# Second attention of a four-stage block: row sums of the softmax on TensorE, division of the heads at the end

## The chip, the cores and the metric

The kernel runs on one core of a Trainium2 chip. The metric is the device time of one execution in microseconds (us). Before the change the median of 3 runs is 1199.65 us (1196.87 to 1201.66).

## The reference

Sixteen batches of 256 rows of width 256 pass through four stages, each added to x: an attention over 77 context rows, a feed-forward layer, a second attention, and a soft mixture of experts. Only the second attention is touched. Cut to it:

```python
q = layernorm(x) @ w_q            # 16 heads of 16 columns
k, v = split(ctx @ w_kv)          # 77 context rows
logits = q k^T * SCALE + (i - j) * w_rel[head]
attn = softmax(logits, axis=-1)   # exp(l - max) / sum
x = x + concat_heads(attn @ v) @ w_proj
```

## The kernel before

The second attention is `attention1`. It is written out without a loop: stage `f` runs from -2 to 17, and within a stage a step `t` runs from 0 to 7. One pair of heads `t` of batch `f` is handled per step; the later parts of batch `f-1` and `f-2` and the preparation of batch `f+1` and `f+2` are laid between the steps. Each engine executes its own list strictly in the order written, and semaphores tie the lists together. So the order of the work is that of the five loops at the end of each engine's block.

What happens to a batch, by function and line of the profile:

- DVE computes the layer norm (`ln.statistics`, L331; `ln.normalise`, L351, which writes `xn`), PE transposes it (`transpose_x`, L942), ACT rounds it (`transposed_x`, L1041, `xT_hi`) and DVE takes the rest (L1115, `xT_lo`). PE makes the queries from both (`queries`, L952). They go over DRAM into another layout (SP's queue, `q_dram`, `att_qs`).
- Step by step: `scores` (PE, L967, two matmuls of 154 columns into `s_bank`), `find_maxima` (DVE, L1127), `exponentials` (ACT, L1059, four activations of 77 columns into `ex`). The row sums are taken in two ways: for even steps DVE adds them up (`add_up`, L1133), for odd steps ACT's accumulator does. `invert` (DVE, L1142) takes the reciprocals of 4 sums a partition, and `weigh` (POOL, L1203 and L1204) multiplies exponentials by them into `prob` (64 of the 77 keys) and `tails` (13).
- Five units a batch (steps 0, 1, 3, 4, 6 of the next stage) move the probabilities to the other side: `transpose_p` (PE, L983, L979), `round_probs` (ACT, L1068, `pT_hi`), `split_probs` (DVE, L1148, `pT_lo`), `weigh_values` (PE, L1004). The last one makes for each of a unit's two chunks three matmuls of 256 columns: values hi with probabilities hi and lo, values lo with hi (PASSES), accumulated in the left half of one of two banks `o_bank`.
- `round_heads` (ACT, L1073) and `split_heads` (DVE, L1153) take the finished heads out of `o_bank`, `project` (PE, L1016) multiplies by `w_proj`, and `add_residual` (DVE, L1159) adds to x.

DVE's loop for a stage, cut:

```python
for t in range(HP):
    find_maxima(f, t)
    if n % 2 == 0: add_up(...)
    if t == 1: split_heads(f - 2, 1)
    if t == 2: split_queries(f + 1)
    invert(...)
    if t in UNIT_AT: split_probs(f - 1, UNIT_AT[t])
    if t == 0: transposed_x(f + 1)
    if t == 7: split_heads(f - 1, 0)
    if t == 5: add_residual(f - 2); ln.statistics(dve, f + 2)
    if t == 7: ln.normalise(dve, f + 2, xt_psum, 1)
```

Of the kernel before, what the change touches and what calls it, by code (L numbers as in the profile page):

```python
# [19 lines left out]
ALU = mybir.AluOpType  # L20
# [769 lines left out]
def attention1(nc, d, st):  # L790
# [7 lines left out]
    with ExitStack() as stack:  # L798
# [18 lines left out]
        rsum = [m.sb(f"rsum{i}", [P, 2 * NC]) for i in range(RING)]  # L817
        rinv = [m.sb(f"rinv{i}", [P, 2 * NC]) for i in range(RING)]
# [17 lines left out]
        vmain_zero = m.sem("vmain_zero")  # L836
# [7 lines left out]
        sum_ready, inv_ready, p_ready = m.sem("sum_ready"), m.sem("inv_ready"), m.sem("p_ready")  # L844
# [22 lines left out]

        def sums_added(n):
            return n // 2 + 1
# [66 lines left out]
        def _(pe):  # L936
# [50 lines left out]
            def weigh_values(g, u):  # L987
                n = UNITS * g + u
                pe.wait_ge(pt_lo, n + 1)
                if u == 0:  # L990
                    pe.wait_ge(vals_ready, VALS * (g + 1))
                    at_least(pe, ot_lo, DC * (g - 1) + 1)
                if u == 2:
                    at_least(pe, ot_lo, DC * g)
                for j in range(2):
                    o = j if u == TAIL_UNIT else CHUNKS[u][j] // 4
                    for k, (a, b) in enumerate(PASSES):
# [6 lines left out]
                        last = nc.tensor.matmul(o_bank[o][:, 0:N], values, pT[n % 2][b][0:rows, j * N:(j + 1) * N],  # L1004
                                                start=u in (0, 2) and j == 0 and k == 0,
                                                stop=k == 2 and ((u == TAIL_UNIT and j == 0) or (u == 4 and j == 1)))
# [31 lines left out]
        def _(act):  # L1038
# [12 lines left out]
            def exponentials(f, t):  # L1051
# [3 lines left out]
                if t % 2 == 0:  # L1055
                    at_least(act, sum_ready, sums_added(n - RING))
                for r in range(2 * NC):
                    total = {} if t % 2 == 0 else dict(accum_out=rsum[t % RING][:, r:r + 1])
                    last = nc.scalar.activation(ex[t % RING][:, r, :], s_bank[t % 2][:, r * SK:(r + 1) * SK], ACT.Exp,  # L1059
                                                bias=mx[t % 2][:, r:r + 1], **total)  # L1060
# [18 lines left out]
            for f in STAGES:  # L1079
                for t in range(HP):  # L1080
# [5 lines left out]
                    if t == 0 and here(f - 2):  # L1086
                        round_heads(f - 2, 1)
# [6 lines left out]
                    if t == 6 and here(f - 1):  # L1094
                        round_heads(f - 1, 0)

        @block.vector
        def _(dve):
# [31 lines left out]
            def add_up(f, t):  # L1130
                n = HP * f + t
                dve.wait_ge(ex_ready, n + 1)
                nc.vector.tensor_reduce(rsum[t % RING][:, :], ex[t % RING][:, :, :], AX, ALU.add).then_inc(sum_ready, 1)  # L1133

            def invert(f, t):
                n = HP * f + t
                if t % 2 == 0:
                    dve.wait_ge(sum_ready, sums_added(n))
                else:
                    dve.wait_ge(ex_ready, n + 1)  # L1140
                at_least(dve, p_ready, 2 * (n - RING + 1))
                nc.vector.reciprocal(rinv[t % RING][:, :], rsum[t % RING][:, :]).then_inc(inv_ready, 1)  # L1142

# [7 lines left out]
            def split_heads(g, j):  # L1151
                dve.wait_ge(ot_hi, DC * g + j + 1)
                nc.vector.tensor_tensor(oT[1][:, j, :], o_bank[j][:, 0:N], fp32_of(oT[0][:, j, :]),  # L1153
                                        ALU.subtract).then_inc(ot_lo, 1)
# [980 lines left out]
```

## Time and profile before

| | |
|---|---|
| median of 3 runs | 1199.65 us |
| the profiled execution | 1201.5 us, of which the span of its one core 1199.7 us |
| busy over the span | PE 1020.2 us (85%), DVE 883.1 (74%), ACT 751.3 (63%), POOL 470.3 (39%) |
| second attention, first to last work | about 702 to 956 us of the span |
| granted clock of TensorE, mean | 0.944 |

The table is read as follows. The share of busy time is a mean over stages with different limits; the change touches one stage, so that the stage's own rows count. Durations in the rows are those of single instructions and overlap a little with their neighbours: on DVE the next instruction starts some 0.08 us before the one ahead of it has ended in the record. So what an instruction costs its engine is the distance from its start to the next one's start. In the steady part of the stage one batch follows the other at a fixed distance, here called the turn: the distance between two batches' `split_queries`, at 766.31, 780.20 and 794.08 us of the span, is 13.88 us.

### The profile page before, as it was taken

The page shows a single profiled execution, that of the slowest core. Times are in us where ns is not written, and L with a number is a line of the kernel's source. Part 1 is how long each engine was busy: PE and PEld are TensorE (multiplying, and loading weights), DVE is VectorE, ACT ScalarE, POOL GpSimd, SP SyncE. Part 2 cuts the span into 40 slices and gives each one's busy share as a digit, 9 for nine tenths or more (in the row PEclk, how much of TensorE's full clock was granted, in tenths as well). Part 3 has the DMA queues.
Part 4 walks back from the last instruction along what each step waited for, and adds up shares of the span by engine and source line. Part 5 has one row for each costly group of instructions (what it writes and reads, how often), then busy time and mean ns, then how long its engine had stood idle before and what let it go on. Part 6 is the DMA issues. An engine that isn't in the chain of part 4 may idle for free. (4 is left out here: it accounts for less than half of the span.)

```text
span 1199.7 us, 27786 instructions
## 1 busy us (share of the span) xinstructions
PE 1020.2 (85%) x8021; PEld 977.4 (81%) x8021; DVE 883.1 (74%) x2261; ACT 751.3 (63%) x2515; POOL 470.3 (39%) x801
## 2 busy tenths in 40 slices
PE   6779999999999999799999947888888637777578
PEld 6679999999999998699999946787887627677567
DVE  3567767777776676677777747999998668986776
ACT  3467666666666666433333338999898527777774
POOL 0132232322323222112121126667676467663655
PEclk9889999999999999899999966999999959999789
DMA  7678970000000000100000035555556050000003
GB/s 216 152 134 218 145 122 0 0 0 0 0 0 0 0 0 1 32 1 0 0 0 0 0 109 150 154 157 164 154 152 171 13 110 2 1 2 1 1 18 122
DMA packets 72190, 75.04 MB, mean 63 GB/s; under 512 B 22608, under 2 KB 64436, under 8 KB 71988
## 3 DMA queue, kind: packets, MB, share of 16 engines
q1 hardware_dynamic: 71300, 73.52, 24.8%
q10 hardware_dynamic: 816, 0.66, 0.2%
q8 instruction: 32, 0.52, 0.2%
q14 instruction: 42, 0.34, 0.1%
HBM read 42.58 MB, written 31.54 MB: 62 GB/s over the span
## 5 line engine op out<-in xcount | busy, mean ns | idle before, releaser
L776 POOL TENSOR_TENSOR att_prob<-att_ex,att_rinv 128x308 f32<-128x308 f32 x128 | 89.9, 702 | 215.8 <-DVE att_rinv L679 202.4
L1059 ACT ACTIVATE att_ex<-att_s_bank,att_mx 128x77 f32<-128x77 f32 x512 | 143.1, 340 | 13.7 <-DVE att_mx L1127 12.2
L1346 ACT ACTIVATE ffn_hid<-ffn_h_bank,ffn_b 128x256 f32<-128x256 f32 x128 | 60.6, 474 | 125.3 <-DVE ffn_hT_lo L1377 65.3
L638 ACT ACTIVATE att_ex<-att_s_bank,att_mx 128x77 f32<-128x77 f32 x512 | 124.7, 332 | 11.5 <-DVE att_mx L669 11.4
L646 ACT ACTIVATE att_qT<-att_q_bank 128x256 f32<-128x256 f32 x128 | 49.1, 384 | 101.2 <-PE att_q_bank L496 100.2
L702 DVE TENSOR_TENSOR att_pT_lo<-att_t_bank,att_pT_hi 128x512 fp32r<-128x512 f32 x128 | 88.3, 690 | 32.2 <-ACT att_pT_hi L616 31.8
L1203 POOL TENSOR_TENSOR att_prob<-att_ex,att_rinv 128x256 f32<-128x256 f32 x128 | 79.8, 623 | 77.2 <-DVE att_rinv L1142 77.1
L516 PE MATMUL att_s_bank<-att_keys,att_qT 128*128 128x154 f32 x512 | 94.9, 308 | 0.0
L616 ACT CAST att_pT_hi<-att_t_bank 128x512 fp32r<-128x512 f32 x128 | 74.9, 586 | 24.4 <-PE att_t_bank L526 19.3
L540 PE MATMUL att_o_bank<-att_pT_hi,att_vals_hi 128*128 128x256 f32 x256 | 83.0, 324 | 3.0 <-DVE att_oT_lo L683 2.0
L967 PE MATMUL att_s_bank<-att_ks,att_qs 100*128 100x154 f32 x256 | 53.2, 292 | 34.3 <-ACT att_ex L1059 17.4
L1317 PE MATMUL ffn_o_bank<-ffn_w_hi,ffn_hT_hi 128*128 128x256 f32 x256 | 74.3, 290 | 7.8 <-DVE ffn_hT_lo L1377 7.8
L683 DVE TENSOR_TENSOR att_oT_lo<-att_o_bank,att_oT_hi 128x256 fp32r<-128x256 f32 x128 | 54.3, 424 | 33.1 <-ACT att_oT_hi L651 29.6
L496 PE MATMUL att_q_bank<-att_xT_hi,att_wq_hi 128*128 128x256 f32 x256 | 75.6, 295 | 2.9 <-DVE att_xT_lo L662 2.9
L526 PE MATMUL att_t_bank<-all_ident,att_prob 128*128 128x128 f32 x512 | 76.5, 272 | 0.0
L1304 PE MATMUL ffn_h_bank<-ffn_xT_hi,ffn_w_hi 128*128 128x256 f32 x256 | 72.6, 283 | 3.5 <-DVE ffn_xT_lo L1364 3.5
L967 PEld LDWEIGHTS att_s_bank<-att_ks,att_qs 100*128 100x128 f32 x256 | 42.1, 205 | 40.4 <-DMA att_qs<-q_dram 31.2
L1127 DVE TENSOR_REDUCE att_mx<-att_s_bank 128x4 f32<-128x308 f32 x128 | 59.7, 466 | 20.3 <-PE att_s_bank L967 20.2
L516 PEld LDWEIGHTS att_s_bank<-att_keys,att_qT 128*128 128x128 f32 x512 | 73.2, 193 | 1.0
L496 PE MATMUL att_q_bank<-att_xT_hi,att_wq_lo 128*128 128x256 f32 x256 | 73.4, 287 | 0.0
L496 PE MATMUL att_q_bank<-att_xT_lo,att_wq_hi 128*128 128x256 f32 x256 | 73.1, 286 | 0.0
L1304 PE MATMUL ffn_h_bank<-ffn_xT_lo,ffn_w_hi 128*128 128x256 f32 x256 | 72.2, 282 | 0.0
(274 smaller groups left out, 4141.3 us busy)
## 6 DMA issues: line engine op xcount, KB each, us to landing
att_qs<-q_dram SPq DMA_DIRECT2D x96, 128.0 KB, 2.8
ks_dram<-att_zeros SPq DMA_DIRECT2D x16, 462.0 KB, 5.7
att_ks<-ks_dram SPq DMA_DIRECT2D x16, 462.0 KB, 4.9
all_x<-in_x SPq DMA_DIRECT2D x4, 1024.0 KB, 7.5
att_vd<-vd_dram SPq DMA_DIRECT2D x16, 256.0 KB
q_dram<-att_qT_hi SPq DMA_DIRECT2D x16, 256.0 KB, 2.1
q_dram<-att_qT_lo SPq DMA_DIRECT2D x16, 256.0 KB, 2.1
out<-comb_y SPq DMA_DIRECT2D x16, 256.0 KB, 2.1
```

Of the source, the lines that this page charges most:

```text
L496: last = nc.tensor.matmul(q_bank[c % 2][:, 0:N], wq[a][:, k, c * P:(c + 1) * P], xT[b][:, k, :], start=n == 0, stop=n == 5)
L516: last = nc.tensor.matmul(out, qT[c % 2][:, q * P:(q + 1) * P], keys[:, kc, h0:h0 + 2, :], start=first, stop=True)
L526: last = nc.tensor.transpose(t_bank[t % 2][:, h * N + q * P:h * N + (q + 1) * P], prob[:, q, (2 * t + h) * SK:(2 * t + h) * SK + P], st.id ...
L540: last = nc.tensor.matmul(o_bank[j % 2][:, 0:N], vals[a][:, v * P:(v + 1) * P], pT[t % 2][b][:, h * N:(h + 1) * N], start=t % PC == 0 and ...
L616: nc.scalar.copy(pT[t % 2][0][:, :], t_bank[t % 2][:, :]).then_inc(pt_hi, 1)
L638: last = nc.scalar.activation(ex[t % RING][:, r, :], s_bank[t % 2][:, r * SK:(r + 1) * SK], ACT.Exp, bias=mx[t % 2][:, r:r + 1])
L702: nc.vector.tensor_tensor(pT[t % 2][1][:, :], t_bank[t % 2][:, :], fp32_of(pT[t % 2][0][:, :]), ALU.subtract).then_inc(pt_lo, 1)
L776: nc.gpsimd.tensor_tensor(out, e, w, ALU.mult).then_inc(p_ready, 1)
L967: last = nc.tensor.matmul(s_bank[t % 2][:, q * PAIR:(q + 1) * PAIR], qs[i][0:ROWS, t, q * P:(q + 1) * P], ks[i][0:ROWS, t // 4, t % 4, :, ...
L1059: last = nc.scalar.activation(ex[t % RING][:, r, :], s_bank[t % 2][:, r * SK:(r + 1) * SK], ACT.Exp, bias=mx[t % 2][:, r:r + 1], **total)
L1203: nc.gpsimd.tensor_tensor(main, e[:, :, :, 0:MAIN], w.to_broadcast([P, NC, 2, MAIN]), ALU.mult).then_inc(p_ready, 1)
L1304: last = nc.tensor.matmul(h_bank[t % 4][:, 0:N], w1[a][:, k, t, :], xT[b][:, k, :], start=n == 0, stop=n == 5)
```

## The change

The probabilities are no longer normalised before they are transposed. GpSimd packs the plain exponentials (`pack`, a copy in place of `weigh`). PE gets the row sums too: behind the three matmuls with values it runs two more (hi and lo part of the exponentials) with a pattern of ones in place of the values, which leaves in the right half of `o_bank` the sum of each head, repeated over the 16 columns of that head. A matmul of 512 columns with weights of zero opens each of the two banks. `add_up` and `invert` and ACT's accumulator reads go. DVE takes the reciprocal of the right half (128 partitions x 256) and multiplies the left half by it into `heads` (`normalise_heads`); ACT rounds `heads` and GpSimd takes the rest (`split_heads`, before on DVE). `key1` and `val1` are given back before the feed-forward stage, which makes room for the new tiles.

```diff
+        ones_main = m.sb("ones_main", [P, 4 * 160], F32R)
+        no_values = m.sb("no_values", [P, P], F32R)
+        ones_tail = m.sb("ones_tail", [P, P], F32R)
+        inv = [m.sb(f"inv{j}", [P, N]) for j in range(DC)]
+        heads = [m.sb(f"heads{j}", [P, N]) for j in range(DC)]
...
                 if u == 0:
                     pe.wait_ge(vals_ready, VALS * (g + 1))
-                    at_least(pe, ot_lo, DC * (g - 1) + 1)
+                    at_least(pe, heads_ready, DC * (g - 1) + 1)
                 if u == 2:
-                    at_least(pe, ot_lo, DC * g)
+                    at_least(pe, heads_ready, DC * g)
+                if u in (0, 2):
+                    nc.tensor.matmul(o_bank[u // 2][:, 0:2 * N], no_values[:, :], pT[n % 2][0][:, 0:2 * N], start=True, stop=False)
...
+                    for b in range(2):
+                        last = nc.tensor.matmul(o_bank[o][:, N:2 * N], ones, pT[n % 2][b][0:rows, j * N:(j + 1) * N], start=False,
+                                                stop=b == 1 and ((u == TAIL_UNIT and j == 0) or (u == 4 and j == 1)))
...
             def round_heads(g, j):
-                act.wait_ge(pv_done, UNITS * g + 4 + j)
+                act.wait_ge(heads_ready, DC * g + j + 1)
                 at_least(act, proj_psum, g)
-                nc.scalar.copy(oT[0][:, j, :], o_bank[j][:, 0:N]).then_inc(ot_hi, 1)
+                nc.scalar.copy(oT[0][:, j, :], heads[j][:, :]).then_inc(ot_hi, 1)
...
+            def normalise_heads(g, j):
+                dve.wait_ge(pv_done, UNITS * g + 4 + j)
+                nc.vector.reciprocal(inv[j][:, :], o_bank[j][:, N:2 * N]).then_inc(inv_ready, 1)
+                dve.wait_ge(inv_ready, DC * g + j + 1)
+                at_least(dve, ot_lo, DC * (g - 1) + j + 1)
+                nc.vector.tensor_tensor(heads[j][:, :], o_bank[j][:, 0:N], inv[j][:, :], ALU.mult).then_inc(heads_ready, 1)
...
-                    if 0 <= n < HP * B and n % 2 == 0:
-                        add_up(n // HP, n % HP)
                     if t == 1 and here(f - 2):
-                        split_heads(f - 2, 1)
+                        normalise_heads(f - 2, 1)
...
-                    if 0 <= n < HP * B:
-                        invert(n // HP, n % HP)
...
                     if t == 7 and here(f - 1):
-                        split_heads(f - 1, 0)
+                        normalise_heads(f - 1, 0)
...
-                pool.wait_ge(inv_ready, n + 1)
+                pool.wait_ge(ex_ready, n + 1)
...
-                nc.gpsimd.tensor_tensor(main, e[:, :, :, 0:MAIN], w.to_broadcast([P, NC, 2, MAIN]), ALU.mult).then_inc(p_ready, 1)
+                nc.gpsimd.tensor_copy(main, e[:, :, :, 0:MAIN]).then_inc(p_ready, 1)
...
+            def split_heads(g, j):
+                pool.wait_ge(ot_hi, DC * g + j + 1)
+                nc.gpsimd.tensor_tensor(oT[1][:, j, :], heads[j][:, :], fp32_of(oT[0][:, j, :]), ALU.subtract).then_inc(ot_lo, 1)
```

On GpSimd `split_heads(f - 2, 0)` stands in step 0 behind `pack`, `split_heads(f - 2, 1)` in step 2; on ACT `round_heads` of half 0 moves from step 6 of stage `f-1` to step 0 of the next, and half 1 from step 0 to step 2, ahead of `round_queries`.

DVE, around the end of a stage (step 7, then steps 0 and 1), before:

```order
L1127 TENSOR_REDUCE att_mx<-att_s_bank 128x4
L1142 RECIPROCAL att_rinv<-att_rsum 128x4
L1153 TENSOR_TENSOR att_oT_lo<-att_o_bank,att_oT_hi 128x256
L351 TENSOR_SCALAR att_xn<-all_x,att_mean_var,att_rstd 128x256 x2
L1127 TENSOR_REDUCE att_mx<-att_s_bank 128x4
L1133 TENSOR_REDUCE att_rsum<-att_ex 128x4
L1142 RECIPROCAL att_rinv<-att_rsum 128x4
L1148 TENSOR_TENSOR att_pT_lo<-att_t_bank,att_pT_hi 128x512
L1115 TENSOR_TENSOR att_xT_lo<-att_xq_bank,att_xT_hi 128x512
```

and after:

```order
L1134 TENSOR_REDUCE att_mx<-att_s_bank 128x4
L1146 RECIPROCAL att_inv<-att_o_bank 128x256
L1149 TENSOR_TENSOR att_heads<-att_o_bank,att_inv 128x256
L351 TENSOR_SCALAR att_xn<-all_x,att_mean_var,att_rstd 128x256 x2
L1134 TENSOR_REDUCE att_mx<-att_s_bank 128x4
L1141 TENSOR_TENSOR att_pT_lo<-att_t_bank,att_pT_hi 128x512
L1122 TENSOR_TENSOR att_xT_lo<-att_xq_bank,att_xT_hi 128x512
L1134 TENSOR_REDUCE att_mx<-att_s_bank 128x4
L1146 RECIPROCAL att_inv<-att_o_bank 128x256
L1149 TENSOR_TENSOR att_heads<-att_o_bank,att_inv 128x256
```

The small reciprocals and the sum are gone; a reciprocal of 256 elements a partition stands in step 7 between the last maximum and `xn`, and a second one in step 1.

PE, step 5 (the unit that opens the second bank), after:

```order
L968 MATMUL att_s_bank<-att_ks,att_qs 128x154 x2
L999 MATMUL att_o_bank<-att_pT_hi,att_no_values 128x512
L1013 MATMUL att_o_bank<-att_pT_hi,att_vmain_hi 128x256
L1013 MATMUL att_o_bank<-att_pT_lo,att_vmain_hi 128x256
L1013 MATMUL att_o_bank<-att_pT_hi,att_vmain_lo 128x256
L1015 MATMUL att_o_bank<-att_pT_hi,att_ones_main 128x256
L1015 MATMUL att_o_bank<-att_pT_lo,att_ones_main 128x256
L1013 MATMUL att_o_bank<-att_pT_hi,att_vmain_hi 128x256
L1013 MATMUL att_o_bank<-att_pT_lo,att_vmain_hi 128x256
L1013 MATMUL att_o_bank<-att_pT_hi,att_vmain_lo 128x256
L1015 MATMUL att_o_bank<-att_pT_hi,att_ones_main 128x256
L1015 MATMUL att_o_bank<-att_pT_lo,att_ones_main 128x256
```

Before, the same place held the two matmuls of `scores` and the six with values; four with ones and the one with `no_values` are new. Every unit gets the four, units 0 and 2 also the one.

## Rows read from the trace of the kernel before

**Rows 1.** Windows of one turn each: stretch and length, busy by engine, PEclk, DMA
```profile
766.30:780.20 13.90, 11.51 (x97) 10.82 (x96) 13.09 (x38) 12.91 (x59) 9.90 (x22) 1.00 0.63 165
780.20:794.10 13.90, 11.45 (x97) 10.84 (x96) 13.10 (x38) 12.93 (x59) 9.91 (x22) 1.00 0.56 165
...
836.50:851.70 15.20, 12.89 (x96) 12.37 (x96) 13.15 (x38) 13.01 (x59) 9.89 (x22) 0.89 0.50 150
...
sum 171.10, PE 143.49 PEld 135.29 DVE 157.34 ACT 155.11 POOL 118.79; mean PE 11.96 PEld 11.27 DVE 13.11 ACT 12.93 POOL 9.90
```

**Rows 2.** Waits from 740 to 920 us: who waited, for whom, total, times, longest
```profile
POOL att_prob L1203 <- DVE att_rinv L1142: 55.3, 38, 3.6
PEld att_s_bank L967 <- DMA att_qs<-q_dram: 20.0, 13, 2.2
...
PE att_s_bank L967 <- ACT att_ex L1059: 10.7, 9, 1.3
```

**Rows 3.** Timeline of DVE: start, duration, line, what, [idle before <-releaser]
```profile
773.39 0.47 DVE L1127 TENSOR_REDUCE att_mx<-att_s_bank 128x4 f32<-128x308 f32 x1
773.78 0.17 DVE L1142 RECIPROCAL att_rinv<-att_rsum 128x4 f32<-128x4 f32 x1
773.86 0.39 DVE L1153 TENSOR_TENSOR att_oT_lo<-att_o_bank,att_oT_hi 128x256 fp32r<-128x256 f32 x1
774.17 1.13 DVE L351 TENSOR_SCALAR att_xn<-all_x,att_mean_var,att_rstd 128x256 f32<-128x256 f32 x2
775.22 0.47 DVE L1127 TENSOR_REDUCE att_mx<-att_s_bank 128x4 f32<-128x308 f32 x1
...
776.77 0.68 DVE L1115 TENSOR_TENSOR att_xT_lo<-att_xq_bank,att_xT_hi 128x512 fp32r<-128x512 f32 x1
...
779.42 0.48 DVE L1127 TENSOR_REDUCE att_mx<-att_s_bank 128x4 f32<-128x308 f32 x1 [0.58 <-PE att_s_bank L967]
```

**Rows 4.** Timeline of PE over the same turn
```profile
775.36 0.66 PE L942 MATMUL att_xq_bank<-all_ident,att_xn 128*128 128x128 f32 x4 [0.27 <-DVE att_xn L351]
...
777.51 0.38 PE L952 MATMUL att_xq_bank<-att_xT_hi,att_wq_hi 128*128 128x256 f32 x1 [0.86 <-DVE att_xT_lo L1115]
777.73 0.28 PE L952 MATMUL att_xq_bank<-att_xT_lo,att_wq_hi 128*128 128x256 f32 x1
...
779.04 0.34 PE L967 MATMUL att_s_bank<-att_ks,att_qs 100*128 100x154 f32 x2
...
785.70 0.45 PE L967 MATMUL att_s_bank<-att_ks,att_qs 100*128 100x154 f32 x2
787.74 0.45 PE L967 MATMUL att_s_bank<-att_ks,att_qs 100*128 100x154 f32 x2 [1.59 <-DMA att_qs<-q_dram]
```

**Rows 5.** Groups by form, DVE's reciprocals in the whole span
```profile
L1142 DVE RECIPROCAL att_rinv<-att_rsum 128x4 f32<-128x4 f32 x128 | 22.0, 172 | 1.7
...
L1675 DVE RECIPROCAL route_rinv<-route_rsum 128x2 f32<-128x2 f32 x32 | 5.3, 166 | 12.9 <-ACT route_ex L1614 11.9
...
L1660 DVE RECIPROCAL route_inv_length<-route_length_min 128x2 f32<-128x2 f32 x16 | 2.4, 147 | 0.8 <-POOL route_length_min L1761 0.5 <-issue 0.3
...
L1717 DVE RECIPROCAL route_mu_inv<-route_mu_max 128x2 f32<-128x2 f32 x1 | 0.1, 131 | 0.0
```

**Rows 6.** Groups by form, 740 to 920 us, ACT's reads and DVE
```profile
L1059 ACT ACTIVATION_READ_ACCUMULATOR att_ex<-att_s_bank,att_mx 128x1 f32 x204 | 42.9, 210 | 0.0
...
L1148 DVE TENSOR_TENSOR att_pT_lo<-att_t_bank,att_pT_hi 128x512 fp32r<-128x512 f32 x51 | 34.1, 669 | 0.3 <-ACT att_pT_hi L1068 0.2
...
L1133 DVE TENSOR_REDUCE att_rsum<-att_ex 128x4 f32<-128x308 f32 x51 | 23.5, 462 | 0.0
...
L1153 DVE TENSOR_TENSOR att_oT_lo<-att_o_bank,att_oT_hi 128x256 fp32r<-128x256 f32 x25 | 10.1, 405 | 0.0
```

**Rows 7.** Groups by form, POOL, a product with a mask and a plain copy
```profile
L1214 POOL TENSOR_TENSOR att_vmain_lo<-att_vd,all_head_mask 128x256 fp32r<-128x256 f32 x16 | 9.8, 613 | 0.0
...
L751 POOL CAST att_vals_hi<-kv_val 77x128 fp32r x13 | 3.7, 287 | 0.0
```

More of the change, by code:

```diff
@@ L816, in attention1 @@
         ex = [m.sb(f"ex{i}", [P, 2 * NC, SK]) for i in range(RING)]
-        rsum = [m.sb(f"rsum{i}", [P, 2 * NC]) for i in range(RING)]
-        rinv = [m.sb(f"rinv{i}", [P, 2 * NC]) for i in range(RING)]
+        ones_main = m.sb("ones_main", [P, 4 * 160], F32R)
[3 more added lines that the diff above has]
+        heads = [m.sb(f"heads{j}", [P, N]) for j in range(DC)]
         prob = m.sb("prob", [P, NC, HP * P])
@@ L991, in weigh_values @@
                     pe.wait_ge(vals_ready, VALS * (g + 1))
-                    at_least(pe, ot_lo, DC * (g - 1) + 1)
+                    at_least(pe, heads_ready, DC * (g - 1) + 1)
                 if u == 2:
-                    at_least(pe, ot_lo, DC * g)
+                    at_least(pe, heads_ready, DC * g)
+                if g == 0 and u == 0:
+                    pe.wait_ge(ones_ready, 3)
+                if u in (0, 2):
+                    nc.tensor.matmul(o_bank[u // 2][:, 0:2 * N], no_values[:, :], pT[n % 2][0][:, 0:2 * N], start=True, stop=False)
                 for j in range(2):
                     o = j if u == TAIL_UNIT else CHUNKS[u][j] // 4
+                    if u == TAIL_UNIT:
+                        ones, rows = ones_tail[0:TAILS, :], TAILS
+                    else:
+                        ones, rows = ones_main[:, (CHUNKS[u][j] % 4) * P:(CHUNKS[u][j] % 4 + 1) * P], P
                     for k, (a, b) in enumerate(PASSES):
@@ L1003, in weigh_values @@
                             values, rows = vmain[g % 2][a][:, at:at + P], P
-                        last = nc.tensor.matmul(o_bank[o][:, 0:N], values, pT[n % 2][b][0:rows, j * N:(j + 1) * N],
-                                                start=u in (0, 2) and j == 0 and k == 0,
-                                                stop=k == 2 and ((u == TAIL_UNIT and j == 0) or (u == 4 and j == 1)))
+                        nc.tensor.matmul(o_bank[o][:, 0:N], values, pT[n % 2][b][0:rows, j * N:(j + 1) * N], start=False, stop=False)
+                    for b in range(2):
+                        last = nc.tensor.matmul(o_bank[o][:, N:2 * N], ones, pT[n % 2][b][0:rows, j * N:(j + 1) * N], start=False,
+                                                stop=b == 1 and ((u == TAIL_UNIT and j == 0) or (u == 4 and j == 1)))
                 last.then_inc(pv_done, 1)
@@ L1086, in _ @@
                     if t == 0 and here(f - 2):
+                        round_heads(f - 2, 0)
+                    if t == 2 and here(f - 2):
                         round_heads(f - 2, 1)
@@ L1093, in _ @@
                         place_positions(1)
-                    if t == 6 and here(f - 1):
-                        round_heads(f - 1, 0)
         @block.vector
@@ L1128, in find_maxima @@
                                         ALU.max, negate=True).then_inc(mx_ready, 1)
[L1130 to L1142, printed above, removed]
             def split_probs(g, u):
@@ L1229, in _ @@
                     if 0 <= n < HP * B:
-                        weigh(n // HP, n % HP)
+                        pack(n // HP, n % HP)
+                    if t == 0 and here(f - 2):
+                        split_heads(f - 2, 0)
+                    if t == 2 and here(f - 2):
+                        split_heads(f - 2, 1)
                     if t == 5 and here(f + 2) and f + 2 > 0:
@@ L2098, in build @@
                 attention0(nc, d, st)
-            ffn(nc, d, st)
-            attention1(nc, d, st)
+        ffn(nc, d, st)
+        attention1(nc, d, st)
         moe(nc, d, st, out)
```

29 lines of the change are left out of this document (13 added, 16 removed).

## The prediction

> **What bounds the kernel now.** The change touches the second attention alone, so I read that stage and take the rest of the span as it is. First the windows of one turn (one batch) each [rows 1]: a clean turn takes 13.88 us, and in it DVE is busy 13.1 us, ACT 12.9, PE 11.5 and POOL 9.9. What the reader is to see is that two engines are nearly full and none has much room. Other turns are longer, as the one from 836.50 with 15.2 us; there the granted clock is 0.89 in place of 1.00, a mixture of TensorE's 2.4 and 1.2 GHz. The twelve turns of rows 1 sum to 171.1 us, 14.26 a turn; twelve clean ones would take 166.6, so that the slow clock costs 4.5 us.
>
> Next the waits [rows 2]. POOL waits for the reciprocals of DVE (55.3 us), which costs nothing as long as POOL is not late. PE waits for exponentials (10.7 us) and for the queries that come back from DRAM (20.0 us on the weight load's side). Then the two timelines of one turn [rows 3, 4], which give the order in which the engines release each other around the end of a stage. DVE makes the maximum of step 7, the heads and `xn` (to 775.22); PE transposes `xn` at 775.36 after a pause of 0.27 us; ACT and DVE split it (`xT_lo` at 776.77), and the queries start at 777.51 after a pause of 0.86. From there PE runs almost without a gap to the scores of step 7 at 785.70, and has a third pause of 1.59 before the next step 0. The ring is closed: scores of step 7, DVE to the end of `xn`, PE's steps 0 to 7.
>
> **The change, part by part.** I walk this ring once with the new instructions. T = 0 is the end of `xn`, 775.22 in rows 3.
>
> PE. Each unit gets four matmuls of 256 columns with ones. Twelve of that size stand between 777.51 and 779.04, and after the first they come every 0.12 us ((779.04 - 777.73)/11) [rows 4]. So the twenty of a batch cost 2.40 us. The two of 512 columns with zero weights have no row of their size; I take two small ones each, 0.24 (as the least one small one, 0.12), together 0.48. PE gets 2.88 us of work a turn, against pauses of 0.27, 0.86 and 1.59, 2.72 together [rows 4]. Of the new work 0.48 us (unit 4, step 0) falls ahead of the transposes of `xn`, where the pause of 1.59 covers it. The other 2.40 us fall between queries and the scores of step 7. There PE has no pause in the record, and I add them in full. Scores of step 7 then start at (785.70 - 775.22) + 2.40 = 12.88.
>
> DVE. It loses four sums and eight small reciprocals a batch, 4 x 0.46 + 8 x 0.17 = 3.2 us of busy time [rows 5, 6]. In the part of the ring on DVE only one small reciprocal (0.08, 773.78 to 773.86) lay, the rest was beside PE's steps 1 to 6. The maximum of step 7 starts 0.38 after its scores (779.04 to 779.42) and takes 0.39 (773.39 to 773.78). Then comes the new reciprocal over 256 elements, R, with some 0.03 until the product that waits for it starts; the product as long as `oT_lo`, 0.31 (773.86 to 774.17), and `xn` 1.05 (774.17 to 775.22) [rows 3, 4]. The turn is 12.88 + 0.38 + 0.39 + R + 0.03 + 0.31 + 1.05 = 15.04 + R.
>
> R decides, and no row has a large reciprocal. From below: one pass over 256 elements out of PSUM is 0.405 us [rows 6]; nothing suggests that a division is quicker than a subtraction. From above: 147 ns for two elements and 172 for four give 12.5 ns an element, 252 x 12.5 + 172 = 3.3 us [rows 5]. The 32 of two elements at 166 ns would give only 3 ns an element, 0.93 us. I take the mean over all 49 of two elements, 159 ns ((32 x 166 + 16 x 147 + 131)/49): (172 - 159)/2 = 6.4 ns an element, R = 1.8 us. The turn is then 16.84 us, 2.96 more than a clean one.
>
> The second reciprocal (step 1) lies between `xT_lo` and `pT_lo` of unit 1. PE needs that `pT_lo` for its weighing in step 3, some 3.7 us after the queries start (1.53 us of queries, step 2, then scores and transposes); DVE, from the same point, has a maximum of 0.39, R, the product's 0.3 and `pT_lo` of 0.6 ahead of it, 3.1 us. So with R = 1.8 it hides beside the queries and step 2, with 0.6 to spare; if that cover were gone it would cost R too. `round_heads` of half 1 stands ahead of `round_queries` on ACT and waits for this product, so the queries leave for DRAM up to 1 us later; the longer turn gives them that time, and I cost it at nothing.
>
> ACT. Four steps a batch lose four accumulator reads each, 16 x 0.21 = 3.4 us of busy time [rows 6]. ACT is nowhere last in the ring, so it gives nothing. POOL. Packing gets cheaper (a copy of 128 elements takes 287 ns, a product of 256 takes 613) and two `split_heads` of some 0.6 come, 1.2 a turn at most [rows 7]. With 9.9 of 13.9 us busy it has room, and half 1 must be ready only by step 4.
>
> Number of turns. Stages 1 to 15 have scores, units and heads together, 15 turns: 15 x 2.96 = 44.4 us. The end gets the last two divisions one after the other: R + 0.03 and 0.2 for POOL in DVE's place (0.61 against 0.41 us) in the last, and about as much for the two before, of which weighing hides a part. The first stage loses sums and accumulator reads, some 1 us. I take +3.5 for both (0 to 6). The slow clock is left as it is: PE is busy 11.5 + 2.9 of 16.8 us, much the same share as now, with longer pauses before `xn`. The sum is +48 us on the profiled execution of 1201.5 us, 1249.5. That one lies 1.85 above the median, so in terms of the median the forecast is **1247.6 us**.
>
> **A rule against the trace.** The small reciprocals differ by 6.4 ns an element in the mean of rows 5, with single differences of 3 and 12.5, which is more than the 1.0 ns that one pass costs (669 - 405 ns for 256 elements, rows 6). The Trainium skill, "VectorE: DVE Perf Modes", section "First, the fixed hardware budget", says that the reciprocal is an iterated division with a repeat count of 8. Read as eight passes an element, the sum by that rule is that of the first rival; read as something inside one pass, it is that of the second.
>
> **The rivals.**
> Eight passes. A pass over 256 elements is 669 - 405 = 264 ns [rows 6], eight are 2.11, with 0.14 of fixed time R = 2.25. The turn is 17.29, 15 x 3.41 = 51 us, with 4 at the ends 1254.8 us. For it: the slope of rows 5 is well over one pass. Against: its mean is below eight.
>
> One pass. R = 0.4, the turn 15.44, PE nearly full and bound by its own work. 15 x 1.56 + 1 = +24 us, 1224; if the clock then stays up through the stage, 4.5 less, 1219. For it: the pair 166 and 172 ns, and the start distance of 0.08 us of a small reciprocal. Against: 131 and 147.
>
> A longer one. R = 3.3, the turn 18.3, and the second reciprocal overruns its cover by 0.9: 15 x 5.3 + 7 = +87, 1286.
>
> Not slower: PE's pauses take everything. If PE gets its new work into pauses that the lighter DVE and ACT no longer cause, the turn is 13.88 + (2.88 - 2.72) = 14.04, and with the clock up all the time this stands against the mean of 14.26: 15 x -0.22 = -3.3, 1196.4 us. It decides when R is under 0.5 and scores, `xn` and `xT_lo` come without a wait. For it: DVE and ACT are the fullest engines and both get lighter. Against: two of the three pauses are latency of the chain from `xn` over ACT and DVE to the queries, which the change does not shorten. A smaller form, R = 0.4 with a matmul pitch under 0.12, would end within 0.5% of 1200.
>
> **How the numbers follow.** Chances: forecast (R from 1.3 to 2.1) 0.41, eight passes 0.22, one pass 0.17, longer 0.07, not slower 0.09 (of it 0.03 faster by over 0.5%), something between one pass and no change 0.04 (half of it within 0.5%). The range leaves out the longest R and the cases around no change, 0.2 in all: from 1216 (one pass with the clock up, less 3 for the ends) to 1262 (eight passes, +7 for the ends and for a slower clock in the longer pauses). The forecast's own range is 1238 to 1253. A measurement of this kernel tells 0.5%, 6 us, from no change. Faster 0.03, same 0.08, slower 0.89.
>
> **What would show it.** In the profile after: a RECIPROCAL of 128x256 on DVE, 32 of them, whose mean is R; turns of 15.04 + R between two `split_queries`; a new wait of PE's transposes (`xq_bank` from `xn`) for `xn` on DVE, of about R each time, while today's 0.27 is the whole of it; PE busy up by some 45 us by pitch; POOL's wait for reciprocals gone; DVE's busy time a turn near 13.1 - 1.8 - 1.4 + 2 x 1.8 = 13.5. The ring is wrong if PE waits in steps 2 to 6, or if the turn is long while `xn` is not waited for. The sum is wrong above all if R is not 1.8: each 0.1 us of it is worth 1.5 us.

## The result, and the profile after

The changed kernel takes 1241.16 us (median of 4 runs, 1239.11 to 1241.64), the kernel before on the same chip 1199.41. The ratio is 1.0346, with a 95% interval from 1.032 to 1.0371: slower by 3.5%. The forecast was 1247.6 us, with a range from 1216 to 1262. The profiled execution took 1241.05 us, with a span of 1239.2 us against 1199.7 before.

The first part of the page of the kernel after gives, for each engine, busy time, share of the span and number of instructions:

```profile
PE 1066.0 (86%) x8373; PEld 1023.6 (83%) x8373; DVE 901.4 (73%) x2101; ACT 734.6 (59%) x2259; POOL 456.1 (37%) x837
```

PE got 45.8 us of work (it had 1020.2), DVE 18.3 (883.1), while ACT lost 16.7 (751.3) and POOL 14.2 (470.3).

The windows of one turn each in the kernel after, with the columns of [rows 1]; the sum is that of 13 turns:

```profile
854.22:870.45 16.23, 14.19 (x107) 13.48 (x106) 14.19 (x27) 11.78 (x41) 8.88 (x25) 0.91 0.49 141
870.45:888.20 17.75, 15.70 (x130) 15.05 (x129) 14.38 (x27) 11.89 (x41) 8.95 (x25) 0.99 0.43 129
888.20:904.41 16.21, 14.16 (x118) 13.51 (x118) 14.18 (x27) 11.78 (x41) 8.88 (x25) 1.00 0.50 141
904.41:920.65 16.24, 14.19 (x118) 13.54 (x118) 14.19 (x27) 11.78 (x41) 8.88 (x25) 1.00 0.50 140
920.65:936.89 16.24, 14.20 (x119) 13.54 (x118) 14.20 (x28) 11.78 (x41) 8.89 (x25) 1.00 0.50 141
...
sum 216.91, PE 190.30 PEld 181.53 DVE 184.67 ACT 153.79 POOL 114.36; mean PE 14.64 PEld 13.96 DVE 14.21 ACT 11.83 POOL 8.80
```

The reader sees a clean turn of 16.24 us in place of 13.88, and no engine that fills it: PE and DVE are each busy 14.2 us of it. A turn that is longer than its fullest engine by 2 us points to a ring of waits.

The waits of the kernel after from 740 to 960 us name the ring (columns as in [rows 2]):

```profile
POOL att_oT_lo L1197 <- ACT att_oT_hi L1080: 54.4, 26, 2.2
...
ACT att_oT_hi L1080 <- DVE att_heads L1149: 22.2, 26, 1.0
...
PE att_xq_bank L943 <- DVE att_xn L351: 13.0, 13, 1.0
...
PE att_xq_bank L953 <- DVE att_xT_lo L1122: 9.9, 13, 0.8
...
PE att_s_bank L968 <- ACT att_ex L1066: 3.7, 13, 0.4
...
PEld att_s_bank L968 <- DMA att_qs<-q_dram: 0.4, 1, 0.4
```

POOL's wait for reciprocals is gone. PE's wait for the exponentials is a third of what it was, and its wait for the queries from DRAM (20.0 us in [rows 2]) has shrunk to a single one of 0.4 us. In their place PE's transposes wait for `xn`, 1.0 us in each of the 13 turns, where it was 0.27 [rows 4].

The timeline of DVE in the kernel after, over the same place as [rows 3]:

```profile
927.37 0.69 DVE L1141 TENSOR_TENSOR att_pT_lo<-att_t_bank,att_pT_hi 128x512 fp32r<-128x512 f32 x1 [0.37 <-ACT att_pT_hi L1075]
928.12 0.48 DVE L1134 TENSOR_REDUCE att_mx<-att_s_bank 128x4 f32<-128x308 f32 x1
928.51 1.75 DVE L1146 RECIPROCAL att_inv<-att_o_bank 128x256 f32<-128x256 f32 x1
930.29 0.42 DVE L1149 TENSOR_TENSOR att_heads<-att_o_bank,att_inv 128x256 f32<-128x256 f32 x1
930.64 0.73 DVE L351 TENSOR_SCALAR att_xn<-all_x,att_mean_var,att_rstd 128x256 f32<-128x256 f32 x2
931.28 0.47 DVE L1134 TENSOR_REDUCE att_mx<-att_s_bank 128x4 f32<-128x308 f32 x1
...
932.73 0.69 DVE L1122 TENSOR_TENSOR att_xT_lo<-att_xq_bank,att_xT_hi 128x512 fp32r<-128x512 f32 x1 [0.38 <-ACT att_xT_hi L1051]
933.34 0.47 DVE L1134 TENSOR_REDUCE att_mx<-att_s_bank 128x4 f32<-128x308 f32 x1
933.72 1.75 DVE L1146 RECIPROCAL att_inv<-att_o_bank 128x256 f32<-128x256 f32 x1
```

and that of PE:

```profile
925.68 0.28 PE L1015 MATMUL att_o_bank<-att_pT_hi,att_ones_main 128*128 128x256 f32 x1
925.80 0.28 PE L1015 MATMUL att_o_bank<-att_pT_lo,att_ones_main 128*128 128x256 f32 x1
...
927.73 0.35 PE L968 MATMUL att_s_bank<-att_ks,att_qs 100*128 100x154 f32 x2
...
930.14 0.28 PE L1015 MATMUL att_o_bank<-att_pT_lo,att_ones_main 128*128 128x256 f32 x1
931.42 0.66 PE L943 MATMUL att_xq_bank<-all_ident,att_xn 128*128 128x128 f32 x4 [1.00 <-DVE att_xn L351]
...
933.47 0.39 PE L953 MATMUL att_xq_bank<-att_xT_hi,att_wq_hi 128*128 128x256 f32 x1 [0.76 <-DVE att_xT_lo L1122]
```

Here the ring can be walked. DVE ends `xn` at 931.28, one turn earlier at 915.04 (931.28 - 16.24). PE starts the scores of step 7 at 927.73, 12.69 later; DVE their maximum 0.39 later (928.12), the reciprocal 0.39 after that (928.51), the product 1.78 after that (930.29), `xn` 0.35 later (930.64), and it is done 0.64 later (931.28). The sum is 16.24, as it must be for steps taken from one clean turn; what it shows is how the turn is divided. During the reciprocal PE still weighs unit 4 (its last matmul starts at 930.14), and then has nothing until `xn` is there.

**Where 39.5 us of span went.** The pitches of 13 turns, from the third on, add up to 216.91 us against 184.52 before: +32.4. Of that 13 x 2.36 = 30.7 is the clean turn (16.24 against 13.88) and 1.7 more slow clock. From 768 to 888 us every second turn is 17.4 to 17.8 long. The low clock stands in the window ahead of such a turn (0.90 or 0.91 from 854.22, 0.99 from 870.45): it falls just ahead of `split_queries`, near 867 us, and is back near 871, and PE's delay shows only in the turn behind. From the last `split_queries` to PE's last weighing it takes 34.16 us where it took 28.28, 5.9 more, of which two clean turns would be 4.7. The first two turns got shorter together by 2.4 (14.50 and 13.05 against 14.86 and 15.11), since there only the accumulator reads and sums were removed. The last batch's heads give 3.6. These are PE's last weighing and the first matmuls behind the heads, first in the kernel before:

```profile
951.80 0.39 PE L1004 MATMUL att_o_bank<-att_pT_hi,att_vmain_hi 128*128 128x256 f32 x1 [0.69 <-DVE att_pT_lo L1148]
...
953.69 0.39 PE L1016 MATMUL att_proj_bank<-att_wo_hi,att_oT_hi 128*128 128x256 f32 x1 [0.92 <-DVE att_oT_lo L1153]
```

and in the kernel after:

```profile
987.27 0.38 PE L1013 MATMUL att_o_bank<-att_pT_hi,att_vmain_hi 128*128 128x256 f32 x1 [0.21 <-DVE att_pT_lo L1141]
...
992.75 0.58 PE L1026 MATMUL att_proj_bank<-att_wo_hi,att_oT_hi 128*128 128x256 f32 x1 [4.04 <-POOL att_oT_lo L1197]
993.13 0.41 PE L1026 MATMUL att_proj_bank<-att_wo_lo,att_oT_hi 128*128 128x256 f32 x1
```

This distance is 5.48 us; it was 1.89 before. Behind the pause of 4.04 us the granted clock is 0.50, the matmuls of the last projection come every 0.21 us and no longer every 0.12, and the last residual is 1.3 us further from the projection's start (2.97 against 1.70). What lies ahead of the first `split_queries` is 0.4 shorter, and what lies behind the last residual 0.8. With that nothing is left over: 32.4 - 2.4 + 5.9 + 3.6 + 1.3 - 0.4 - 0.8 = 39.6, the 39.5 but for rounding.

### The profile page after: what moved, and what is told of

The parts are those of the page before. It is cut to its first block and busy times, and to the rows that moved or that the text cites. A ratio compares the mean times of both kernels' runs of the same rounds, so it can differ in the third digit from the quotient of the medians.

```text
span 1239.2 us, 28016 instructions
## 1 busy us (share of the span) xinstructions
PE 1066.0 (86%) x8373; PEld 1023.6 (83%) x8373; DVE 901.4 (73%) x2101; ACT 734.6 (59%) x2259; POOL 456.1 (37%) x837
## 5 line engine op out<-in xcount | busy, mean ns | idle before, releaser
L1066 ACT ACTIVATE att_ex<-att_s_bank,att_mx 128x77 f32<-128x77 f32 x512 | 125.9, 341 | 18.8 <-DVE att_mx L1134 17.7
L638 ACT ACTIVATE att_ex<-att_s_bank,att_mx 128x77 f32<-128x77 f32 x512 | 125.0, 333 | 11.5 <-DVE att_mx L669 11.2
L1141 DVE TENSOR_TENSOR att_pT_lo<-att_t_bank,att_pT_hi 128x512 fp32r<-128x512 f32 (+1 forms) x80 | 55.0, 688 | 26.0 <-ACT att_pT_hi L1075 26.0
L1308 PE MATMUL ffn_h_bank<-ffn_xT_hi,ffn_w_lo 128*128 128x256 f32 x256 | 72.1, 282 | 0.0
L540 PE MATMUL att_o_bank<-att_pT_lo,att_vals_hi 128*128 128x256 f32 x256 | 72.0, 281 | 0.0
```

Source lines behind the costliest of these rows:

```text
L540: last = nc.tensor.matmul(o_bank[j % 2][:, 0:N], vals[a][:, v * P:(v + 1) * P], pT[t % 2][b][:, h * N:(h + 1) * N], start=t % PC == 0 and ...
L1308: last = nc.tensor.matmul(h_bank[t % 4][:, 0:N], w1[a][:, k, t, :], xT[b][:, k, :], start=n == 0, stop=n == 5)
```

## Experiments

The theory was the ring of the prediction, with R = 1.75 known by then: the reciprocal of step 7 and the PE work both stand in it, the reciprocal of step 1 doesn't. The rivals were DVE's total (both reciprocals count alike), and PE's total (the turn is PE's work plus fixed pauses, and DVE doesn't matter). All ratios are to the kernel before on the same chip; the changed kernel stands at 1.0346.

**Reciprocal of step 7 replaced by a copy**

```diff
-                nc.vector.reciprocal(inv[j][:, :], o_bank[j][:, N:2 * N]).then_inc(inv_ready, 1)
+                if j == 0:
+                    nc.vector.tensor_copy(inv[j][:, :], o_bank[j][:, N:2 * N]).then_inc(inv_ready, 1)
+                else:
+                    nc.vector.reciprocal(inv[j][:, :], o_bank[j][:, N:2 * N]).then_inc(inv_ready, 1)
```

> The changed kernel, but the division of half 0 (step 7) is a plain copy of the sums, one pass in place of the reciprocal; the heads of half 0 come out multiplied by their sums, not divided. Ring theory (scores of step 7, then maximum, reciprocal, product and xn on DVE, then PE's steps): the reciprocal stands in the ring, 1.75 us become some 0.4, the turn falls from 16.24 to about 15.0, where PE's unit 4 becomes last. 15 turns: 1241 goes to 1219 to 1224 us. Rival A (DVE is bound by its total of busy time): the same 1.35 a turn, 1221. Rival B (PE's new matmuls bound it, the reciprocal is beside them): 1238 to 1241.

Measured: 1219.07 us, 1.0129 (1.0107 to 1.015). A turn of this kernel, by its windows:

```profile
798.04:813.04 15.00, 13.96 (x118) 13.51 (x118) 12.86 (x27) 11.65 (x41) 8.86 (x25) 1.00 0.53 153
```

The turn is 15.00, the slow clock has gone from all 13 turns. 1.24 us less a clean turn is nearly the 1.33 by which the instruction got shorter. This refutes PE's total, by which DVE doesn't matter (1238 to 1241). The ring and DVE's total both forecast this number; the next run divides them.

**Reciprocal of step 1 replaced by a copy**

The edit is given against the kernel of the first experiment; the reciprocal of step 7 is back.

```diff
-                if j == 0:
+                if j == 1:
```

> The changed kernel, but the division of half 1 (step 1) is a plain copy; the heads of half 1 come out multiplied by their sums. Ring theory: this reciprocal runs beside PE's queries and step 2 and is free but for the last one of the stage: 1238 to 1241 us. Rival A (DVE's total of busy time): 1.35 a turn as in the other half, 1221. Rival B: 1238 to 1241.

Measured: 1235.99 us, 1.027 (1.0251 to 1.0289).

```profile
751.83:768.03 16.20, 14.15 (x119) 13.50 (x118) 13.12 (x28) 11.83 (x41) 8.88 (x25) 1.00 0.49 141
```

The clean turns stay at 16.20 to 16.22, though DVE has 1.07 us less to do in each. So this reciprocal costs nothing in a clean turn, though it is as long as the other. That refutes DVE's total. (That 13 turns add up to 216.77 us against 216.91 is partly chance: the first of them is 1.1 shorter, and more of the others are slow.) The median, a little under the 1238 to 1241 expected, is lower than the changed kernel's by 0.76%, some 9 us, which is more than the ends explain: the profiled execution, the slowest of the four with 1240.19 us, shows only 0.7 us at the last batch (its last residual starts at 994.99 against 995.72). The rest isn't in any row and stays open. With step 7 already a copy, the same edit takes 3.7 us (the next experiment against the first, 1.0098 against 1.0129), where 15 turns of 1.35 would have been 20.

**Both replaced**

Again against the first experiment:

```diff
-                if j == 0:
+                if True:
```

> The changed kernel with both divisions as plain copies; all heads come out multiplied by their sums. Ring theory: as with half 0 alone, less the end: 1216 to 1222 us, turn about 15.0. Rival A: twice 1.35 a turn, 1200. Rival B: 1238 to 1241.

Measured: 1215.56 us, 1.0098 (1.0077 to 1.0119).

```profile
796.61:811.61 15.00, 13.96 (x119) 13.51 (x118) 11.79 (x27) 11.75 (x41) 8.89 (x25) 1.00 0.54 153
```

The turn is the same 15.00 as with one copy, while DVE's work fell by another 1.07 us. With both divisions priced at a copy the change is still slower than the kernel before: what is left is PE's work and the copies themselves, 0.42 us each.

**Row sums taken out of PE**

The matmuls with ones are left out, and the opening one gets weights of one.

```diff
-                    for b in range(2):
-                        last = nc.tensor.matmul(o_bank[o][:, N:2 * N], ones, pT[n % 2][b][0:rows, j * N:(j + 1) * N], start=False,
...
-            pool.memset(fp32_of(no_values[:, :]), 0.0).then_inc(ones_ready, 1)
+            pool.memset(fp32_of(no_values[:, :]), 1.0).then_inc(ones_ready, 1)
```

> The changed kernel without the matmuls with the pattern of ones; the 512-column matmul that opens a bank stays and has weights of one in place of zero, so that the right half is a finite number (the sums and heads are not the reference's). Both reciprocals stay. Ring theory: 16 of the 20 matmuls lie between queries and scores of step 7, 16 x 0.12 = 1.9 us a turn go, 15 turns: 1241 - 29 = 1212 us. Rival A (DVE's total): 1238 to 1241. Rival B (PE's matmuls alone): all 2.4 us a turn, 1205.

Measured: 1237.37 us, 1.0277 (1.0255 to 1.0299), far from the 1212 us expected. Two turns of this kernel:

```profile
834.65:851.58 16.93, 14.60 (x98) 13.73 (x97) 14.11 (x27) 12.05 (x41) 8.83 (x25) 0.80 0.47 134
...
885.29:900.56 15.27, 12.39 (x102) 11.58 (x101) 13.99 (x27) 11.85 (x41) 8.84 (x25) 1.00 0.52 150
```

The number alone would fit DVE's total (1238 to 1241), which the copies have refuted. Two things went otherwise than in the ring's forecast. The clean turn is 15.27, 0.97 shorter and not 1.92: PE caught up with the others and waits for exponentials, as its timeline in the turn after this one shows,

```profile
901.74 0.42 PE L968 MATMUL att_s_bank<-att_ks,att_qs 100*128 100x154 f32 x2 [0.42 <-ACT att_ex L1064]
...
906.33 0.35 PE L968 MATMUL att_s_bank<-att_ks,att_qs 100*128 100x154 f32 x2
907.71 0.42 PE L968 MATMUL att_s_bank<-att_ks,att_qs 100*128 100x154 f32 x2 [1.02 <-ACT att_ex L1064]
...
910.36 1.11 PE L943 MATMUL att_xq_bank<-all_ident,att_xn 128*128 128x128 f32 x4 [1.09 <-DVE att_xn L351]
```

and DVE's has

```profile
906.10 0.46 DVE L1132 TENSOR_REDUCE att_mx<-att_s_bank 128x4 f32<-128x308 f32 x1
```

The first wait goes back to DVE, where the maximum of step 2 stands behind the reciprocal of step 1. The second goes back to the maximum of step 6, which starts at 906.10 behind the residual and the statistics; it lies behind the scores of step 7 (906.33) and so outside the ring. In the ring, from `xn` (894.95 us) to those scores PE takes 11.38 in place of 12.69, 1.31 less. Their maximum then starts at 907.07, behind `pT_lo`, 0.74 later and not 0.39. Together that is the 0.97, but for rounding. And most turns are of the first kind: with a granted clock of 0.80 to 0.88 they are 16.0 to 17.0 us long, about as slow as with the ones.

**`xn` ahead of the division in step 7**

```diff
-                    if t == 7 and here(f - 1):
-                        normalise_heads(f - 1, 0)
...
                     if t == 7 and here(f + 2) and f + 2 > 0:
                         ln.normalise(dve, f + 2, xt_psum, 1)
+                    if t == 7 and here(f - 1):
+                        normalise_heads(f - 1, 0)
```

> The changed kernel with the two pieces of step 7 on DVE exchanged: xn is made ahead of the division of half 0. PE's transposes then find xn ready. Ring theory: the reciprocal stays in the ring by another way, since ACT rounds half 0 ahead of x, and DVE has division, maximum and pT_lo ahead of xT_lo: from the end of the maximum of step 7 to the start of xT_lo 3.85 us in place of 4.2. About 0.4 a turn, 6 us of 1241 go, ratio to the kernel before 1.029. Rival (only the wait of the transposes for xn costs, 1.0 us a turn): 15 us less, ratio 1.022. Clock rival: as now, or worse.

Measured: 1232.14 us, 1.0268 (1.0243 to 1.0294).

```profile
863.91:879.81 15.90, 13.97 (x118) 13.51 (x118) 14.25 (x27) 11.66 (x41) 9.01 (x25) 1.00 0.50 144
```

The turn falls by 0.34 to 15.90, near the 0.4 expected, and the slow clock goes too (1.00 in all 13 turns), which makes the whole gain larger. Why a reciprocal of 1.74 us costs nearly as much behind `xn` as ahead of it is seen in the timelines of this kernel. ACT:

```profile
890.63 0.40 ACT L1080 CAST att_oT_hi<-att_heads 128x256 fp32r<-128x256 f32 x1 [1.41 <-DVE att_heads L1149]
890.94 0.58 ACT L1051 CAST att_xT_hi<-att_xq_bank 128x512 fp32r<-128x512 f32 x1
```

PE:

```profile
892.30 0.39 PE L953 MATMUL att_xq_bank<-att_xT_hi,att_wq_hi 128*128 128x256 f32 x1 [1.66 <-DVE att_xT_lo L1122]
```

PE's wait for `xn` is gone, and its wait for `xT_lo` grew from 0.76 to 1.66. On ACT the rounding of the heads, which waits for the division, stands ahead of the rounding of `xT`, and DVE itself goes from the division (888.40) over product, maximum and `pT_lo` to `xT_lo` (891.55) without a pause. Both come out at the same time (`xT_hi` is done at 891.52), and no run takes one away alone. The division left one link of the ring and stayed ahead of the next.

**Both parts out: no ones, no reciprocals**

```diff
-                    for b in range(2):
-                        last = nc.tensor.matmul(o_bank[o][:, N:2 * N], ones, pT[n % 2][b][0:rows, j * N:(j + 1) * N], start=False,
...
-                nc.vector.reciprocal(inv[j][:, :], o_bank[j][:, N:2 * N]).then_inc(inv_ready, 1)
+                    nc.vector.tensor_copy(inv[j][:, :], o_bank[j][:, N:2 * N]).then_inc(inv_ready, 1)
```

> Both suspected costs taken out of the changed kernel: no matmuls with ones, and copies in place of both reciprocals (no sums and no division in the output). What is left is the gain that the change was to bring: no sums, small reciprocals and accumulator reads. Ring theory: the turn of 15.0 without reciprocals loses the ones too; 1.9 of them in the ring, down to about 13.1, 1188 us, ratio 0.99. If TensorE's clock falls with less work, as it did without the ones alone (0.80), up to 1.2 us a turn comes back, ratio 1.005. Rival (DVE's total, 11.7 us busy a turn now): the same without the clock, 0.98.

Measured: 1190.61 us, 0.9931 (0.9907 to 0.9955).

```profile
870.86:884.29 13.43, 11.63 (x99) 11.07 (x98) 11.66 (x28) 11.83 (x41) 8.92 (x25) 1.00 0.62 169
```

The forecast was 13.1 and 1188. This is what the relief of DVE, ACT and POOL gives here, with the two opening matmuls and the two copies of 0.42 us still in. ACT is 1.1 us and DVE 1.4 us less busy a turn than before, and the turn is 0.44 shorter. PE waits for exponentials and for queries from DRAM, as before the change.

With these kernels the way from one clean turn to the other can be gone part by part: 13.88 before, -0.44 for all that is neither ones nor reciprocals, +1.57 for the ones (15.00 against 13.43), +1.24 for the reciprocal of step 7 over a copy, 0 for that of step 1. These are differences of neighbours, so that they add up to 16.24 by themselves; the sum checks nothing. The prices hold in this order alone: without the ones the two divisions cost 1.84 a turn (15.27 against 13.43), and the ones beside the divisions 0.97 (16.24 against 15.27). Whichever comes second costs 0.60 less, since part of it falls into waits that the first one made.

**A second reciprocal in step 1**

```diff
+                if j == 1:
+                    nc.vector.reciprocal(spare[:, :], o_bank[j][:, N:2 * N])
```

> The changed kernel with a second reciprocal of the same 128x256 in step 1, into a spare tile that nobody reads. Ring theory: in the clean turn of the changed kernel pT_lo of unit 1 is ready at 920.29 and PE's weighing of unit 1 would start at 920.97, a cover of 0.7 us; the second reciprocal adds 1.75, so about 1.1 us a turn come out, turn 17.3, 16 to 20 us more than the changed kernel, ratio to the kernel before 1.048 to 1.052. Rival (DVE's total of busy time, 14.2 + 1.75 = 16 us a turn, still under 16.24): no change, 1.035.

Measured: 1260.17 us, 1.0487 (1.0453 to 1.052).

```profile
912.79:930.31 17.52, 14.69 (x118) 13.61 (x117) 15.80 (x28) 11.67 (x41) 8.89 (x25) 1.00 0.47 130
```

The turn is 1.28 us longer for 1.75 us of work, so that the cover had 0.5 us left; the prediction gave it 0.6. The wait appears where it should, at the weighing behind `pT_lo` of unit 1, among the waits from 740 to 940 us:

```profile
PEld att_o_bank L1014 <- DVE att_pT_lo L1142: 9.9, 10, 1.0
```

**Half of the sums, `xn` first**

Only the hi part of the exponentials is summed, which leaves two ones matmuls out per unit, with the order of the experiment on `xn`.

```diff
-                    for b in range(2):
+                    for b in range(1):
```

> The changed kernel with xn ahead of the division in step 7, and with the ones matmul for the hi part of the exponentials alone: the sums leave out the lo part. Ten ones matmuls a turn go, eight of them in the ring, 0.96 us. Ring theory: turn 15.90 - 0.96 = 14.94, 14 us less than with xn first alone, ratio 1.015. Rival (without the ones alone the ring lost only 0.97 of 1.92, as ACT then waits for the maximum behind step 1's division): about half, 15.4, ratio 1.021; and TensorE's clock may fall.

Measured: 1234.13 us, 1.0261 (1.0226 to 1.0296).

```profile
802.59:818.04 15.45, 13.07 (x96) 12.47 (x95) 14.30 (x27) 11.60 (x41) 9.22 (x25) 0.89 0.53 148
...
834.59:851.28 16.69, 14.31 (x109) 13.80 (x109) 14.35 (x27) 11.78 (x41) 9.06 (x25) 0.91 0.47 137
```

PE's work was cut by 1.2 us a turn (ten matmuls at 0.12) against the kernel with `xn` first, and the time is the same within the intervals. The shortest turns are 15.25 to 15.58 us, most are 16.7, at a granted clock of 0.91 to 0.96 where it was 1.00. With fewer matmuls PE is busy longer, 14.31 us where it was 13.97. So the slow clock took the gain; how large it is at full clock isn't shown, since no turn of this run has the full clock.

**Two edits of the kernel before.** Since the relief of DVE seemed worth something, it was tried without the change: the small reciprocal behind `split_probs`,

```diff
-                    if 0 <= n < HP * B:
-                        invert(n // HP, n % HP)
...
+                    if 0 <= n < HP * B:
+                        invert(n // HP, n % HP)
```

> The kernel before, with the small reciprocal of a step put behind split_probs, so that DVE does not wait for its own sum (0.11 us) ahead of it. If DVE's list is what bounds a turn of 13.88: three such waits a turn go, 0.33 us, 15 turns, 5 us less, ratio 0.996. If ACT (12.9 of 13.9 busy) bounds it as much: no change.

and one reciprocal of 8 elements for two steps:

```diff
-                    if 0 <= n < HP * B:
+                    if 0 <= n < HP * B and n % 2 == 1:
```

> The kernel before, with one reciprocal of 128x8 for two steps in place of two of 128x4; GpSimd waits for the pair. DVE loses four reciprocals (0.08 us each by starts) and four waits for its own sum, gains four elements in each of the others (6.3 ns each, 0.1 us a turn): 0.65 us a turn less if DVE bounds it, 10 us in 15 turns, ratio 0.992. If ACT bounds it: no change or 3 us. GpSimd gets pairs at once and packs up to 1.5 us later, which its slack of 4 us a turn covers.

(The second diff is cut: the sums and reciprocals of two steps share a tile there, and GpSimd waits for pairs.) Measured: 1199.74 us, 0.9996 (0.9979 to 1.0014), and 1197.97 us, 0.9991 (0.9977 to 1.0005). A turn of the first:

```profile
906.96:920.63 13.67, 11.40 (x97) 10.81 (x96) 12.79 (x37) 12.82 (x59) 9.98 (x22) 1.00 0.59 168
```

In both the clean turn is 13.67 in place of 13.88, less than the 0.33 and 0.65 forecast for a turn bound by DVE, and by as much in both; it should still have given 3 us. It is not in the medians: the turns with a granted clock under 0.9, 14.3 to 16.1 us long, are still there. Neither is a difference that this measurement can tell. None of the runs that keep the computation whole beats the kernel before.

## Why the prediction was right

**The ring held.** The prediction gave the turn as 12.88 + 0.38 + 0.39 + R + 0.03 + 0.31 + 1.05. By term the trace shows 12.69, 0.39, 0.39, 1.75 with 0.03 behind it, 0.35 and 0.64. R was taken as 1.8. The two terms that were off are `xn`, 0.41 too long, and PE's part, 0.19 too long (0.10 of it is the pause at `xT_lo`, 0.76 in place of 0.86). The forecast of 16.84 was 0.60 over the 16.24 measured, which is 9.0 us over 15 turns; the ends and the slow clock brought 4.1 where the sum had 3.5. So the profiled execution rose by 39.5 us and not by 48. The median is only 6.4 us under the forecast, because the profiled execution before lay 1.85 above its median and the one after lies on it.

**R.** The groups by form of the kernel after, from 740 to 960 us:

```profile
L1146 DVE RECIPROCAL att_inv<-att_o_bank 128x256 f32<-128x256 f32 x26 | 45.5, 1748 | 0.0
```

Between 4 and 256 elements that is (1748 - 172)/252 = 6.25 ns an element; the prediction took 6.4 (6.46 without its rounding) from one group of four elements against the mean of three groups of two. It was a weak basis (the groups apart gave 3 and 12.5), and its closeness is partly luck. Eight passes of 264 ns would have been 2.25 us, one pass 0.4; the measured duration is neither.

**PE's ones.** They come every 0.12 us as assumed (925.68 to 925.80), and from `xn` to the scores of step 7 the trace has 12.69 where the sum had 12.88. From the queries to those scores PE has no pause in the record, so adding in full fits the stretch. As a price it is too high: the ones cost 1.57 us of a clean turn when nothing else is added (15.00 against 13.43), where exponentials and DMA had left pauses for them, and 0.97 beside the divisions.

**The wait for `xn`.** Predicted as about R, 1.8, measured 1.00. That step was wrong: PE has work left when the maximum of step 7 starts. It weighs unit 4 until some 930.3, and only the rest of the division is seen as a wait. A link of a ring need not appear as a wait of its own length; the experiment with the copy shows that nearly all of its excess over a copy counts (1.24 of 1.33).

**Step 1's reciprocal.** Costed at nothing with 0.6 us of cover to spare, and both halves were tested: taking it away moved no clean turn, doubling it cost 1.28 of 1.75. The later queries cost nothing either, as forecast: PE's wait for them fell to 0.4 us in all.

**ACT and POOL give nothing.** Right in the main: all that was taken off ACT, DVE and POOL is worth 0.44 us a turn when nothing else is added. That it is worth nothing beside ones and divisions is read from the walk, not tested by itself.

**DVE's busy time.** 13.5 forecast, 14.2 measured, though `xn` got shorter. The mistake was to take durations off: a small reciprocal lasts 0.17 but the next instruction starts 0.08 after it [rows 3], and busy time counts the overlap once. Eight of them removed take some 0.65 us away and not 1.4; with the same 0.09 of overlap four sums take 1.5 and not 1.8. 13.1 - 0.65 - 1.5 + 2 x 1.75 - 0.4 for `xn` is 14.05.

**The slow clock.** "Left as is" was nearly right by its size (+1.7 us) but weakly argued, by PE's share of busy time. The forecast compared 11.5 of 13.9 with 14.4 of 16.8 (83% and 86%); the kernel with one copy has none of it at 93% (13.96 of 15.00), and the one without the ones much of it, at 81% in its clean turn (12.4 of 15.3). That the size came out is luck.

**The ends.** +3.5 us were taken for both. Beside 15 clean turns the last heads gave 3.6, the last stages 1.2, the last projection at the low clock 1.3, while the first turns gave 2.4 back and what lies ahead and behind another 1.2: 2.4 together, with rounding, and 1.7 of slow clock in the turns.

**The signs of the rivals.** "Not slower" rested on PE's pauses taking everything; PE did take some, but its two latencies at `xn` and `xT_lo` stayed (1.00 and 0.76). "One pass" is what the experiment with both copies built: 1215.56 us, 1.0098, in turns of 15.00 at the full clock, where the sum gave 15.44 and 1219. The 0.41 of `xn` was too long in that sum too.

## What to carry to other kernels

Before moving a sum or a division, find the closed ring of the stage and ask which new instruction stands in it: here two identical reciprocals of 1.75 us cost 1.24 us a clean turn and nothing, each against a copy, by their places alone. A division over values that repeat pays for every copy: the ones pattern repeats each sum over 16 columns, so DVE divides 256 elements a partition twice, 3.5 us a batch, where 32 elements in 8 small instructions took 0.65 us from start to start. Work taken from an engine that is merely full, but not last in a wait, gives back a fraction of itself (0.44 us of a turn for 1.1 to 1.4 us here).

## What the runs showed of the hardware

**Less work for TensorE, no less time.** Twice PE work was taken out and the granted clock fell: to 0.80 with the ones out (PE waits of 1.02 and 1.09 us in a turn), to 0.91 with half of them out. With `xn` first it stayed at 1.00, and so it did with ones and divisions out, where PE is busy only 11.6 of 13.4 us, less than in either of the two. So it isn't PE's busy time alone. Nor does one program behave alike from turn to turn: in the kernel after, the last turns from 888 us stay at 1.00, and those before them do not. With the ones out the slow turns are 0.8 to 1.7 us longer than the clean one, about what the edit was to bring. What decides between the two levels was not settled.

**`xn` and GpSimd slow each other.** The two TENSOR_SCALARs of `xn` took 1.13 us before, beside products on POOL (774.17 to 775.30 [rows 3]), and 0.73 after, with POOL idle from 929.3 to 931.2. This is one of the products, in the kernel before; it usually takes 0.62:

```profile
774.48 0.67 POOL L1203 TENSOR_TENSOR att_prob<-att_ex,att_rinv 128x256 f32<-128x256 f32 x1
```

In the kernel with `xn` first, copies of POOL run beside them, by its timeline:

```profile
887.35 0.40 POOL L1192 COPY att_prob<-att_ex 128x256 f32<-128x256 f32 x1
...
887.66 0.81 DVE L351 TENSOR_SCALAR att_xn<-all_x,att_mean_var,att_rstd 128x256 f32<-128x256 f32 x2
...
887.86 0.47 POOL L1192 COPY att_prob<-att_ex 128x256 f32<-128x256 f32 x1
```

Both are longer: `xn` takes 0.81, and the copy that falls inside it 0.47 where the one before takes 0.40. The Trainium skill, "SBUF — State Buffer", section "Who interferes with whom", says that VectorE and GpSimd share a pair of ports, that a TENSOR_SCALAR can run in a mode that takes it, and that whoever issues first then has it for the whole instruction while the other is blocked. The rows agree that both lose, but the copy loses 0.07 us, not the length of a TENSOR_SCALAR (0.40). Which mode ran no row shows, and no run changes POOL's work alone. This is the term of the sum that was 0.41 us too long, and a change that moves work on GpSimd should price it.

**The reciprocal.** 6.25 ns an element against 1.03 for a pass [rows 6]: by this estimate it costs as much as six passes. It rests on two sizes, 4 and 256 elements; no run has one between them.
